# First experts of batches 1 to 6 as split float32r products with stationary tokens, turned back by VectorE and SyncE's DMAs

## The reference

```python
def _gemma_mlp(x, gate_w, up_w, down_w):
    g = jnp.einsum('bsh,hi->bsi', x, gate_w)
    u = jnp.einsum('bsh,hi->bsi', x, up_w)
    return jnp.einsum('bsi,ih->bsh', jax.nn.gelu(g, approximate=True) * u, down_w)
...
w, sel = jax.lax.top_k(rw, TOP_K)
w = w / w.sum(axis=-1, keepdims=True)
...
g, u, d, we = params
return (acc + we[:, None, None] * _gemma_mlp(x, g, u, d), None)
```

## Time and profile before

| what | value |
|---|---|
| median of three runs | 85.16 us (84.93, 85.16, 85.42) |
| span of the profiled execution | 83.9 us |
| its own time beside the span | not given apart; the median lies 1.2 us above the span |
| TensorE busy | 81.2 us (97%) |
| VectorE, ScalarE, GpSimd busy | 48.4 us, 31.7 us, 15.8 us |
| GpSimd busy after 32.7 us | 0 |
| granted TensorE clock | 1.00 throughout |
| DMA, mean over the span | 220 GB/s; 290 to 311 GB/s in the batches |

### The profile page before, as it was taken

One profiled execution on the slowest core, in us unless ns is written; L12 is line 12 of the kernel. 1 busy time (PEld: TensorE's weight loads), 2 busy tenths in 40 slices (PEclk: granted clock), 3 DMA queues, 4 the chain that ended last, 5 costly groups with the idle time before them and its releaser, 6 DMA issues.

```text
span 83.9 us, 1866 instructions
## 1 busy us (share of the span) xinstructions
PE 81.2 (97%) x620; PEld 77.4 (92%) x620; DVE 48.4 (58%) x115; ACT 31.7 (38%) x59; POOL 15.8 (19%) x20
## 2 busy tenths in 40 slices
PE   6999999999999999999999999999999999999990
PEld 6979998888889989999999999999999999999990
DVE  1497798835335997428328447466464662842471
ACT  6410995875558400221221221302402402225570
POOL 3020398389666800000000000000000000000000
PEclk9999999999999999999999999999999999999999
DMA  1997000899993000885879798898989989914202
GB/s 13 373 356 284 1 0 0 211 369 347 393 410 152 0 4 0 272 257 228 252 237 408 166 350 331 264 309 356 299 281 319 317 280 307 333 54 135 84 0 63
DMA packets 5335, 18.50 MB, mean 220 GB/s; under 512 B 592, under 2 KB 1744, under 8 KB 5328
## 3 DMA queue, kind: packets, MB, share of 16 engines
q1 hardware_dynamic: 5040, 17.62, 61.3%
q10 hardware_dynamic: 288, 0.79, 2.5%
HBM read 17.88 MB, written 0.52 MB: 219 GB/s over the span
## 4 chain that ended last, share of the span: by engine, by line
PE 97%; DVE 0%; issue 0%
PE bank L697 34%; PE bank L707 17%; PE bank L721 9%; PE bank L736 4%; PE bank L661 4%; PE bank L677 4%; PE bank L669 4%; PE bank L592 3%; PE bank L600 3%; PE bank L684 2%; PE bank L687 2%; PE bank L685 2%; PE bank L630 2%; PE bank L618 2%; PE bank L609 2%; DVE out_sb L511 0%
## 5 line engine op out<-in xcount | busy, mean ns | idle before, releaser
L697 PE MATMUL bank<-x_t,pair_w 128*128 128x128 f32 (+1 forms) x256 | 31.0, 275 | 0.0
L697 PEld LDWEIGHTS bank<-x_t,pair_w 128*128 128x128 f32 x256 | 29.9, 192 | 0.1
L300 ACT ACTIVATE gelu<-bank 128x512 f32<-128x512 f32 x24 | 14.2, 596 | 31.8 <-PE bank L697 27.8
L482 DVE SCALAR_TENSOR_TENSOR hid<-gelu,wsel,bank 128x512 f32<-128x512 f32 x16 | 12.0, 747 | 18.5 <-PE bank L697 18.5
L707 PE MATMUL bank<-hid,pair_w 128*128 128x128 f32 x128 | 17.0, 275 | 0.0
L707 PEld LDWEIGHTS bank<-hid,pair_w 128*128 128x128 f32 x128 | 15.6, 192 | 0.1
L264 POOL TENSOR_TENSOR hid_l<-hid,hid_h 128x512 fp32r<-128x512 f32 x8 | 10.2, 1286 | 4.3 <-ACT hid_h L328 4.3
L480 DVE TENSOR_TENSOR hid<-gelu,bank 128x512 f32<-128x512 f32 x8 | 5.5, 687 | 6.3 <-ACT gelu L300 3.8
L721 PE MATMUL bank<-x_t,w 128*128 128x128 f32 x64 | 8.5, 275 | 0.0
L721 PEld LDWEIGHTS bank<-x_t,w 128*128 128x128 f32 x64 | 7.8, 192 | 0.0
L304 ACT ACTIVATE tanh<-half 128x256 f32<-128x256 f32 x6 | 2.5, 416 | 10.1 <-DVE half L518 10.1
(11 more groups left out here) (70 smaller groups left out, 77.4 us busy)
## 6 DMA issues: line engine op xcount, KB each, us to landing
pair_w<-in_skill SPq DMA_DIRECT2D x16, 768.0 KB, 5.1
w<-in_layer SPq DMA_DIRECT2D x8, 384.0 KB, 5.0
rest_sb<-in_rest SPq DMA_DIRECT2D x1, 661.0 KB, 3.8
x_t<-in_x SPq DMA_DIRECT2D x1, 512.0 KB, 5.3
shared_sb<-in_shared ACTq DMA_DIRECT2D x1, 512.0 KB, 5.1
out_x<-out_sb SPq DMA_DIRECT2D x8, 64.0 KB, 4.4
shared_sb<-in_shared ACTq DMA_DIRECT2D x1, 256.0 KB, 5.3
head_sb<-in_head SPq DMA_DIRECT2D x1, 164.0 KB, 2.4
```

The lines of the kernel that those rows point to most:

```text
L300: act.activation(gelu[:, n, :], ps[:, :], ACT.Gelu_apprx_tanh).then_inc(gelu_ready, 1)
L482: dve.scalar_tensor_tensor(hid[:, n, :], gelu[:, n, :], wsel[:, bass.DynSlice(weight, 1)], u_ps[n][:, :], ALU.mult, ALU.mult).then_inc(hid ...
L697: mm = pe.matmul(ps[:, S * t:S * (t + 1)], pair_w[:, slot, n, 128 * t:128 * (t + 1)], x2_t[:, columns(b)], start=True, stop=True)
```

## The change

For the first experts (k = 0) of batches 1 to 6 (TURNED):

- gate_up_wide takes the place of gate_up. The batch's tokens, already split into x2_h and x2_l, are the stationary operand, and the expert's gate and up weights move, 512 columns at a time: x2_h x wide_h, x2_l x wide_h, x2_h x wide_l, for gate and then for up. The result has tokens on the partitions and the inner width along the free axis.
- The weights' split is new work: ScalarE (round_first) rounds gate and up into wide_h after the first GELU of the batch before, and GpSimd subtracts into wide_l. Both read the weights through by_quadrant, with a step of four elements (16 bytes) between neighbours, so that the columns come to lie in the order in which the later turn puts them right.
- VectorE multiplies into hid as before, and then transposes hid in blocks of 32 x 32 (turn) into turned. SyncE's queue moves the four quadrants of 32 partitions to their places with four DMAs (swap), 64 KB each, from SBUF to SBUF into hid_t, and down(b, 0) reads hid_t.
- down(b, 0) of these batches moves behind down(b, 1), into the next batch: gate_up_wide(b), down(b-1, 1), down(b-1, 0), down3(b-2), gate_up(b, 1), layer 4 of b-1. The residual waits for the later of the two (both_down).
- pair_w becomes first_w with three slots and second_w with two. SyncE reads both expert numbers of a batch ahead of its waits, and issues in batch b: second expert of b+1, the four swaps of b, first expert of b+2 (when down(b-1, 0) has freed its slot), layer-4 weights of b, store of b-2. The first expert of batch 2 is loaded with the first loads.
- The loops of TensorE, ScalarE and VectorE are written out.

The diff, cut to its core (eight leading blanks taken off):

```diff
-pair_w = sb("pair_w", [128, 2 * TOP_K, 3, I])
+first_w, second_w = sb("first_w", [128, 3, 3, I]), sb("second_w", [128, 2, 3, I])
+wide_h, wide_l = sb("wide_h", [128, 2, 2, I], fp32r), sb("wide_l", [128, 2, 2, I], fp32r)
+turned, hid_t = sb("turned", [128, 2, I]), sb("hid_t", [128, 2, I])
...
+def pair_of(b, k):
+    return (first_w[:, b % 3, :, :], first_in[b % 3], b // 3 + 1) if k == 0 else (
+        second_w[:, b % 2, :, :], second_in[b % 2], b // 2 + 1)
+down_order = [(0, 0)]
+for b in range(1, B):
+    down_order += [(b - 1, 1)] + ([(b - 1, 0)] if b - 1 in TURNED else []) + ([] if b in TURNED else [(b, 0)])
+down_order += [(B - 1, 1)]
+def down_at(b, k):
+    return NSH + down_order.index((b, k)) + 1
+def both_down(b):
+    return max(down_at(b, 0), down_at(b, 1))
+def swaps(b):
+    return len([a for a in TURNED if a <= b and a % 2 == b % 2])
+def by_quadrant(ap):
+    return ap.rearrange("p (t i j) -> p j t i", j=T, i=QUAD)
...
@@ -187,14 +217,24 @@
         sp.dma_start(x_t[:, :], x[:, :]).then_inc(x_loaded, 16)
         sp.wait_ge(routed, 1)
-        def load_pair(b, k, q, used=None):
-            slot = TOP_K * q + k
-            e = sp.value_load(chosen[0:1, bass.DynSlice(TOP_K * b + k, 1)], min_val=0, max_val=E - 1)
+        def expert(b, k):
+            return sp.value_load(chosen[0:1, bass.DynSlice(TOP_K * b + k, 1)], min_val=0, max_val=E - 1)
+        def load_pair(b, k, e, used=None):
+            w, landed, _ = pair_of(b, k)
             if used is not None:
                 sp.wait_ge(down_done, used)
-            sp.dma_start(pair_w[:, slot, :, :],
-                         skill[bass.DynSlice(e, 1), :, :, :].rearrange("o p n i -> (o p) n i")).then_inc(pair_in[slot], 16)
+            sp.dma_start(w, skill[bass.DynSlice(e, 1), :, :, :].rearrange("o p n i -> (o p) n i")).then_inc(landed, 16)
+        def swap(b):
+            q = b % 2
+            sp.wait_ge(turned_ready, b - TURNED[0] + 1)
+            if b - 2 in TURNED:
+                sp.wait_ge(down_done, down_at(b - 2, 0))
+            for a in range(T):
+                sp.dma_start(hid_t[:, q, S * a:S * (a + 1)], turned[QUAD * a:QUAD * (a + 1), q, :]).then_inc(swapped[q], 16)
         def load_w3(b, q, used=None):
@@ -209,27 +249,26 @@
             sp.dma_start(out[bass.DynSlice(b, 1), :, :].rearrange("o c s -> (o c) s"),
                          out_sb[:, q, :]).then_inc(stored[q], 16)
-        def refill(b, q, first=True, second=True, before_last=True):
-            if first:
-                load_pair(b + 1, 1, 1 - q, NSH + TOP_K * b)
-            if before_last:
-                load_w3(b, q, b - 1)
-                store(b - 2, q)
-            if second:
-                load_pair(b + 2, 0, q, NSH + TOP_K * b + 1)
         for b in range(2):
             for k in range(TOP_K):
-                load_pair(b, k, b)
+                load_pair(b, k, expert(b, k))
             load_w3(b, b)
-        refill(0, 0, first=False, before_last=False)
-        refill(1, 1, before_last=False)
-        for b in range(2, B - 2):
-            refill(b, b % 2)
-        refill(B - 2, 0, second=False)
-        refill(B - 1, 1, first=False, second=False)
+        load_pair(2, 0, expert(2, 0))
+        load_pair(3, 0, expert(3, 0), down_at(0, 0))
+        for b in range(1, B):
+            if b + 1 < B:
+                second = expert(b + 1, 1)
+            if 2 <= b < B - 2:
+                first = expert(b + 2, 0)
+            if b + 1 < B:
+                load_pair(b + 1, 1, second, down_at(b - 1, 1))
+            if b in TURNED:
+                swap(b)
+            if 2 <= b < B - 2:
+                load_pair(b + 2, 0, first, down_at(b - 1, 0))
+            if b >= 2:
+                load_w3(b, b % 2, b - 1)
+                store(b - 2, b % 2)
         store(B - 2, 0)
         store(B - 1, 1)
...
@@ -264,6 +303,16 @@
             pool.tensor_tensor(hid_l[:, k % 3, :], hid[:, k % 2, :], hid_h[:, k % 3, :].bitcast(fp32),
                                ALU.subtract).then_inc(hid_low, 1)
+        for n, b in enumerate(TURNED):
+            w, _, _ = pair_of(b, 0)
+            for m in range(2):
+                if m == 0 and b - 2 in TURNED:
+                    pool.wait_ge(u_done, NSH + TOP_K * (b - 2) + 1)
+                pool.wait_ge(wide_high, 2 * n + m + 1)
+                pool.tensor_tensor(wide_l[:, b % 2, m, :].rearrange("p (j t i) -> p j t i", j=T, i=QUAD), by_quadrant(w[:, m, :]),
+                                   wide_h[:, b % 2, m, :].bitcast(fp32).rearrange("p (j t i) -> p j t i", j=T, i=QUAD),
+                                   ALU.subtract).then_inc(wide_low, 1)
     @block.scalar
     def _(act):
         act.preload_act_table(ACT.Exp)
...
@@ -315,8 +364,20 @@
             act.wait_ge(x3_ready, b + 1)
             act.activation(x3b[:, q, :], x3_t[:, q, :], ACT.Identity, bias=bsel[:, 2 * HC, b:b + 1]).then_inc(x3b_ready, 1)
+        def round_first(b):
+            w, landed, fill = pair_of(b, 0)
+            act.wait_ge(landed, 16 * fill)
+            if b - 2 in TURNED:
+                act.wait_ge(u_done, NSH + TOP_K * (b - 2) + 1)
+            for m in range(2):
+                act.activation(wide_h[:, b % 2, m, :].rearrange("p (j t i) -> p j t i", j=T, i=QUAD),
+                               by_quadrant(w[:, m, :]), ACT.Copy).then_inc(wide_high, 1)
         def batch(b, last=True):
             gelu_step(NSH + TOP_K * b, 0, g_ps[0])
+            if b + 1 in TURNED:
+                round_first(b + 1)
             gelu_step(NSH + TOP_K * b + 1, 1, g_ps[1])
             if last:
                 tanh_step(b - 1)
@@ -333,11 +394,8 @@
             round_hidden(k - 1)
         round_hidden(NSH - 1)
         batch(0, last=False)
-        batch(1)
-        with act.Fori(1, B // 2 - 1) as j:
-            for q in range(2):
-                batch(2 * j + q)
-        batch(B - 2)
+        for b in range(1, B - 1):
+            batch(b)
         batch(B - 1, last=False)
         act.preload_act_table(ACT.Silu)
         silu_step(B - 2, 0)
...
@@ -472,10 +530,10 @@
             dve.wait_ge(gelu_ready, k + 1)
             dve.wait_ge(u_done, k + 1)
-            if isinstance(k, int) and 2 <= k < NSH + 2:
+            if 2 <= k < NSH + 2:
                 dve.wait_ge(hid_low, k - 1)
-            elif at_least(k, 2):
-                dve.wait_ge(down_done, k - 1)
+            elif k >= NSH + 2 and not (n == 0 and (k - NSH) // TOP_K - 1 in TURNED):
+                dve.wait_ge(down_done, down_at((k - NSH) // TOP_K - 1, n))
             if weight is None:
                 dve.tensor_tensor(hid[:, n, :], gelu[:, n, :], shu_ps(k)[:, :], ALU.mult).then_inc(hid_ready, 1)
             else:
...
@@ -487,9 +545,17 @@
             dve.tensor_tensor(x2s[:, N * h:N * (h + 1)], sh_acc[h][:, :], x2_t[:, N * h:N * (h + 1)],
                               ALU.add).then_inc(x2s_ready, 1)
+        def turn(b):
+            q = b % 2
+            dve.wait_ge(hid_ready, NSH + TOP_K * b + 1)
+            if b - 2 in TURNED:
+                dve.wait_ge(swapped[q], 16 * T * swaps(b - 2))
+            dve.transpose(turned[:, q, :], hid[:, 0, :]).then_inc(turned_ready, 1)
         def residual(b, q):
-            dve.wait_ge(down_done, NSH + TOP_K * (b + 1))
+            dve.wait_ge(down_done, both_down(b))
             if at_least(b, 2):
                 dve.wait_ge(out_ready, b - 1)
             dve.tensor_tensor(x3_t[:, q, :], acc_ps[:, 0:S], x2s[:, columns(b)], ALU.add).then_inc(x3_ready, 1)
@@ -549,6 +615,8 @@
         def batch(b, q, last=True, before_last=True):
             hidden(NSH + TOP_K * b, 0, TOP_K * b)
+            if b in TURNED:
+                turn(b)
             if last:
                 residual(b - 1, 1 - q)
             if before_last:
...
@@ -687,25 +753,43 @@
             pe.matmul(sh_acc[h][:, :], shared_h[:, 2, C * t:C * (t + 1)], hid_l[:, n, :], start=False, stop=(t == T - 1)
                       ).then_inc(down_done, 1)
-        def gate_up(b, k, q):
-            slot, step = TOP_K * q + k, NSH + TOP_K * b + k
+        def gate_up(b, k):
+            step = NSH + TOP_K * b + k
+            w, landed, fill = pair_of(b, k)
             pe.wait_ge(hid_ready, step - 1)
-            pe.wait_ge(pair_in[slot], 16 * fills(b, q))
+            pe.wait_ge(landed, 16 * fill)
             for n, (ps, done) in enumerate(((g_ps[k], g_done), (u_ps[k], u_done))):
                 for t in range(T):
-                    mm = pe.matmul(ps[:, S * t:S * (t + 1)], pair_w[:, slot, n, 128 * t:128 * (t + 1)], x2_t[:, columns(b)],
+                    mm = pe.matmul(ps[:, S * t:S * (t + 1)], w[:, n, 128 * t:128 * (t + 1)], x2_t[:, columns(b)],
                                    start=True, stop=True)
                 mm.then_inc(done, 1)
-        def down(b, k, q):
-            slot, step = TOP_K * q + k, NSH + TOP_K * b + k
-            pe.wait_ge(hid_ready, step + 1)
-            if k == 0 and at_least(b, 1):
+        def gate_up_wide(b):
```

(36 more changed lines are left out.)

43 lines of the change are left out of this document (23 added, 20 removed).

## The result

The changed kernel takes **90.36 us** in the median of four runs (90.03 to 91.4), the kernel before beside it 85.23 (84.93 to 85.42): a ratio of 1.056 (95% interval 1.049 to 1.063), 4.8 us slower. Forecast were 84.9 us, in a range from 83.2 to 87.0.

The account below looks back on a forecast made before the run. TensorE, 97% of the chain, was taken as the bound. From a span of 83.9 us, less 2.55 for shorter products, plus 2.30 for waits, came 83.65; with 1.26 for the median of runs, 84.9 us, range 83.2 to 87.0.

Parts of the forecast that it names:

- The products: On TensorE, six float32r matmuls of 0.23 us replace 16 entries: 1.36 for 1.79 us, 2.55 us saved in all.
- Transpose and subtraction: VectorE's transpose takes 0.70 us (bounds 0.55 and 1.1), each stepped GpSimd subtraction 1.63 us (upper bound 2.09).
- the surcharge taken from VectorE's reduction: Reading weights with a 16-byte step adds 0.34 us over 512 elements, making ScalarE's rounding 0.97 and GpSimd's subtraction 1.63 us.
- The rival of a dearer subtraction: GpSimd's stepped subtraction takes 2.09 us, TensorE waits 4.1 us, and the time is 86.8 us; chance 0.13.
- the loop of 13.7 us: From batch b's last float32r matmul through swaps, load and rounding to b+2's: 13.7 us against 12.54, costing 2.30 in all.
- Four swaps 1.8: SyncE's four swap entries, 0.45 us each, take 1.8 us before the first expert's load is issued at 3.95 us.
- It lands 5.1 later, the median of sixteen: The first expert's load of b+2 lands 5.1 us after issue, at 9.05 us; bounds 4.3 and 5.9.
- with the ends of every term the loop is 11.6 to 14.5 us: Range claimed for the loop spanning two batches; above 12.54 us it counts twice.
- That falls inside the first loop, which waits anyway: Batch 1's swap lands 0 to 1.2 us after down(1, 0) wants it, inside a loop that already waits.
- The queue becomes the bound: Swap bytes raise DMA busy time to 7.0 us, longer than a batch: 86.1 us, up to 87; chance 0.15.
- All is hidden: Stepped reading costs ScalarE and GpSimd nothing, the loop is 12.6 us, as long as two batches: 82.7 us; chance 0.28.

Follow-up runs that it names:

- unawaited swaps: Changed kernel with swaps issued and moved but not awaited by the down product, which reads the transpose's tile: 89.86 us, ratio 1.054.
- the small swaps: Changed kernel, swaps not awaited by the down product, which reads the transpose's tile, and packets of 32 bytes in place of 512: 88.93 us, ratio 1.048.
- the run without waits: Changed kernel without swaps, with contiguous columns for roundings and subtractions, and GpSimd's first wide subtraction waiting for batch 0's hidden half: 83.01 us, ratio 0.976.

## Why the prediction was wrong

- **The products** were right: 0.23 us each, 6.28 us for a batch without waits (6.27 forecast), and 2.0 us for all where nothing waits (2.55; in that profile batch 6 is 0.3 us longer than the others).
- **Transpose and subtraction** were right: 0.711 and 1.54 us for 0.70 and 1.63. The rounding, 0.97 forecast, is 1.14: the surcharge taken from VectorE's reduction was too small for ScalarE. In the loop rounding and subtractions cancel, 4.33 us from the landing to the low half for 4.38. The rival of a dearer subtraction fell: 1.54 against 1.27 contiguous is a fifth more. The Trainium skill, GPSIMD Engine Reference, section Performance pitfalls for Q7 kernels, has half more; the measurement decides.
- **The step that failed is the loop of 13.7 us, in two of its terms.** It is 15.6 us both times, from the last product of batch 2 (40.09) to that of batch 4 (55.68), and from there to that of batch 6 (71.29):

```profile
55.68 0.50 PE L777 MATMUL bank<-wide_l,x_h 128*128 128x512 f32 x1 [0.25 <-POOL wide_l L312]
...
71.29 0.50 PE L777 MATMUL bank<-wide_l,x_h 128*128 128x512 f32 x1 [0.52 <-POOL wide_l L312]
```

  In the second of them the load is issued at 5.06 for 3.95, landed at 11.23 for 9.05, and the low half is there at 15.56 for 13.43. Twice 1.9 us are 3.8 of the 6.5 between the span of this profile and the forecast one (90.1 and 83.65).
  - *"Four swaps 1.8"*, with the conclusion that 5.5 of 6.27 us of SyncE's time fit. An entry of a swap takes 0.64 and not 0.45; the row it was priced by was of loads from HBM. Four take 2.7 us, and the load starts 2.9 after the transpose for the 2.0 forecast. This is 0.9 us of the 1.9. The runs show what the entries weigh: without swaps the two loops are 12.7 and 14.0 us and 4.2 us of the loss go; with unawaited swaps, small or not, at least 3.5 of that come back.
  - *"It lands 5.1 later, the median of sixteen"*. That median mixes first and second experts. The first experts' loads behind a full queue took 5.5 to 5.9 us in the kernel before already, the 5.9 that the prediction gave as its upper bound, and 5.4 to 6.2 in the loops here. It doesn't take the swaps' bytes: with the small swaps the last two took 6.3 and 5.9, and without swaps it is 6.5 in the median. This is the other 1.1 us.
- **The ends of the range** were added up wrongly: "with the ends of every term the loop is 11.6 to 14.5 us". The lower end has every term; the upper has the late landing alone. With the transpose at 1.1 and the subtractions at 2.09 too, the prediction's own upper ends give 15.8, which holds the 15.6 measured.
- **"That falls inside the first loop, which waits anyway"** was half right about the swap of batch 1. Its wait of 2.3 us (0 to 1.2 forecast) stands in the loop from batch 2 to 4. With unawaited swaps that loop is 14.3 us, so half of what the wait costs would have been lost there anyway, and half comes on top. The swap of batch 6, not looked at, stands in no loop and adds 0.95.
- **Missing altogether** was the start: GpSimd's first wide subtractions stand beside VectorE's expert weights. GpSimd's work was costed as time of an idle engine, and only its end was followed. Pk and wnorm in the kernel before, 0.77 us for 128x8 and 128x16 numbers up to the end of an operation of GpSimd's, would have told it. About 1 us. The Trainium skill, SBUF — State Buffer, section SBUF: two separate sides, has the rule: VectorE and GpSimd share a pair of ports, one holds it for its whole instruction, and some kinds of VectorE's operations need it. The runs agree, with 1.21 us beside contiguous subtractions and 1.45 to 1.48 beside stepped ones.
- **The rivals.** "The queue becomes the bound" (0.15) came nearest in its sign and its waits, but not in its reason: it counted bytes, and its upper end was 87. "All is hidden" (0.28) is what the run without waits shows, which leaves the three costs out.

What stays open: why a swap of 64 KB lands 3 to 7 us after its entry; and whether a single entry for all four quadrants, or more tiles for the first experts, would give the queue its slack back. Neither of these two was tried. How the clock's fall is decided is open too.
